# The conditioning nets' first layer moved up between x's first two weight blocks, with its tiles and the class table reordered on the load queue

## What is computed

```python
def _mlp_ln(s, W1, b1, W2, b2, g, b):
    h = jax.nn.silu(s @ W1 + b1) @ W2 + b2
    return _ln(h, g, b)

h = _ln(x, pw_g[pathway_ids], pw_b[pathway_ids])
h = _ln(h, cp_g[compartment_ids], cp_b[compartment_ids])
t = _ln(x, tm_g[time_steps], tm_b[time_steps])
m = x + _mlp_ln(memory_state, mem_W1, ...)[:, None, :]
n = x + _mlp_ln(noise_state, noi_W1, ...)[:, None, :]
r = x + _mlp_ln(resource_state, res_W1, ...)[:, None, :]
s = _ln(x, ms_g[scale_type], ms_b[scale_type])
w = softmax(aw)
cat = concatenate([w[0]*h, w[1]*t, w[2]*m, w[3]*n, w[4]*r, w[5]*s], axis=-1)
out = x + _mlp_ln(cat, int_W1, int_b1, int_W2, int_b2, int_g, int_be)
```

## Time and profile before

| | us |
|---|---|
| median of 3 runs | 929.16 |
| lowest and highest | 928.73, 929.22 |
| the profiled execution | 928.64 |
| its span in the trace | 926.9 |
| TensorE busy in the span | 919.0 |
| VectorE busy | 825.6 |
| ScalarE busy | 326.7 |
| GpSimd busy | 472.5 |

### The profile page before, as it was taken

One profiled execution on the slowest core, in us unless ns is written; L12 is line 12 of the kernel. 1 busy time (PEld: TensorE's weight loads), 2 busy tenths in 40 slices (PEclk: granted clock), 3 DMA queues, 4 the chain that ended last, 5 costly groups with the idle time before them and its releaser, 6 DMA issues.

```text
span 926.9 us, 13511 instructions
## 1 busy us (share of the span) xinstructions
PE 919.0 (99%) x4194; PEld 747.9 (81%) x4194; DVE 825.6 (89%) x1204; ACT 326.7 (35%) x415; POOL 472.5 (51%) x578
## 2 busy tenths in 40 slices
PE   9999999999999999999999999999999999999997
PEld 8777888888888888888888888888888888888885
DVE  7889999899898989989899898989989898998955
ACT  5835234252332514234242333424233251423412
POOL 5556473545545464563645546464563645446141
PEclk9999999999999999999999999999999999999999
DMA  9984757738566583856738465683856748475451
GB/s 333 358 307 148 227 163 244 196 89 279 154 206 179 164 267 102 254 142 234 197 112 281 139 214 161 197 244 91 268 139 239 182 137 276 120 241 145 126 114 45
DMA packets 99619, 178.75 MB, mean 193 GB/s; under 512 B 10129, under 2 KB 49041, under 8 KB 95633
## 3 DMA queue, kind: packets, MB, share of 16 engines
q1 hardware_dynamic: 44512, 95.88, 29.1%
q0 software_dynamic: 22976, 66.07, 27.9%
q10 hardware_dynamic: 32112, 16.58, 6.1%
HBM read 145.75 MB, written 32.75 MB: 193 GB/s over the span
## 4 chain that ended last, share of the span: by engine, by line
PE 97%; DVE 1%; DMA 1%; POOL 1%; ACT 0%; issue 0%; POOLq 0%; DVEq 0%; SPq 0%
PE hid_ps L1620 25%; PE hid_ps L1621 25%; PE hid_ps L1622 25%; PE o_ps L1707 3%; PE o_ps L1706 3%; PE made_ps L1707 3%; PE made_ps L1706 3%; PE o_ps L1708 3%; PE made_ps L1708 3%; PE made_ps L1563 1%; DMA keep<-int_W 1%; PE hid_ps L1627 0%; PE o_ps L1532 0%; PE o_ps L1520 0%; PE o_ps L1521 0%; PE o_ps L1548 0%
## 5 line engine op out<-in xcount | busy, mean ns | idle before, releaser
L1620 PE MATMUL hid_ps<-cat_hi,w_hi 128*128 128x512 f32 x1008 | 394.5, 391 | 0.0
L1622 PE MATMUL hid_ps<-cat_hi,w_lo 128*128 128x512 f32 x1008 | 392.3, 389 | 0.0
L1621 PE MATMUL hid_ps<-cat_lo,w_hi 128*128 128x512 f32 x1008 | 392.3, 389 | 0.0
L1620 PEld LDWEIGHTS hid_ps<-cat_hi,w_hi 128*128 128x128 f32 x1008 | 189.2, 188 | 46.2 <-issue 7.4
L1622 PEld LDWEIGHTS hid_ps<-cat_hi,w_lo 128*128 128x128 f32 x1008 | 189.2, 188 | 39.6
L1621 PEld LDWEIGHTS hid_ps<-cat_lo,w_hi 128*128 128x128 f32 x1008 | 189.3, 188 | 38.5
L617 POOL DMA_INDIRECT pw_rows<-pw,path_now x64 | 73.6, 1149 | 123.4 <-DVE y_sb L1147 106.6
L638 POOL DMA_DIRECT2D r_sb<-x x60 | 57.5, 958 | 108.2 <-DVE r_sb L1225 105.5
L853 ACT ACTIVATE cat_hi<-v_ring 128x1024 fp32r<-128x1024 f32 x30 | 31.9, 1062 | 201.2 <-DMA v_ring<-h_turned 201.2
L624 POOL DMA_INDIRECT pw_rows<-cp,class_now x64 | 84.1, 1313 | 32.7 <-issue 13.0
L845 ACT ACTIVATE cat_hi<-v_ring 128x1024 fp32r<-128x1024 f32 x64 | 66.4, 1059 | 84.1 <-DVE v_ring L1091 37.9
(11 more groups left out here) (199 smaller groups left out, 1385.4 us busy)
## 6 DMA issues: line engine op xcount, KB each, us to landing
x_sb<-xp SPq DMA_DIRECT2D x16, 1024.0 KB
out<-r_sb SPq DMA_DIRECT2D x63, 256.0 KB, 2.0
xc<-xT SPq DMA_DIRECT2D x15, 1024.0 KB, 9.3
h_turned<-y_sb ACTq DMA_DIRECT2D x60, 256.0 KB
r_sb<-x POOLq DMA_DIRECT2D x60, 256.0 KB, 4.2
v_ring<-h_turned SPq DMA_DIRECT2D x60, 256.0 KB
stats_bc<-token_stats SPq DMA_DIRECT2D x15, 512.0 KB
ids_sb<-ids SPq DMA_DIRECT2D x16, 256.0 KB
```

Source lines behind the costliest of these rows:

```text
L1620: pe.matmul(acc, w1_hi[:, k, cols], hi, start=start, stop=False)
L1621: pe.matmul(acc, w1_hi[:, k, cols], lo, start=False, stop=False)
L1622: return pe.matmul(acc, w1_lo[:, k, cols], hi, start=False, stop=stop)
```

## The change

- SyncE's list: the class table (`tabs`, 256 KB) now goes ahead of x^T's second half (512 KB), and the four NET tiles go straight behind it, so ahead of `keep_load(2)`, the ids, `keep_load(3)`, row_ids, blocks 4 and 5 and the kinds. Their wait for `stage_cleared` moves with them.
- TensorE: `nets_hidden` runs behind the second `warm` (13 instead of 15 matmuls) and ahead of `x_high_part(1)`; it writes `made_ps` instead of `o_ps` and doesn't wait for `xhat_copied` any more. `nets_hidden_turn`, which stays where it was, takes that wait. `first_fill(0)`, which writes `made_ps`, waits for `net_hid_rows`.
- ScalarE: the class table's two operations go ahead of `x_high(0, 1)`, and `nets_rows` from behind `w_high(5)` to between `sum_high(1)` and `sum_first(2)`.
- VectorE's new `x_moments`, behind `x_stats` of batch 0, makes variance plus EPS and minus the mean; GpSimd's part for batch 0 is left with two operations of four: the power, and the product with minus the mean.

```diff
-WARM = (30, 15)
+WARM = (30, 13)
...
             keep_load(1)
+            sp.dma_start(tab_raw, tabs).then_inc(table_in, 16)
             load_xT_half()
-            sp.dma_start(tab_raw, tabs).then_inc(table_in, 16)
+            for n in NET:
+                if tiles[n][1] < P:
+
+                    sp.wait_ge(stage_cleared, 1)
+                stage_load(n)
             keep_load(2)
...
-                nth = 1 if isinstance(b, int) and b == 0 else b + 2
-                rstd(xaggr, TT * (b + 1), xve, xve_done, xrs, xrs_done, xmv, slice(0, TT), nth)
                 if isinstance(b, int) and b == 0:
-
+                    pool.wait_ge(xve_done, 2)
+                    pool.tensor_tensor(xrs[:, :], xve[:, :], minus_half[:, :], ALU.pow).then_inc(xrs_done, 1)
                     pool.wait_ge(xrs_done, 1)
-                    pool.tensor_tensor(xmr[:, :], xmv[:, :, 0], xrs[:, :], ALU.mult).then_inc(xve_done, 1)
-                    pool.wait_ge(xve_done, 2)
-                    pool.tensor_tensor(xnmr[:, :], c_zero, xmr[:, :], ALU.subtract).then_inc(xrs_done, 1)
+                    pool.tensor_tensor(xnmr[:, :], xmr[:, :], xrs[:, :], ALU.mult).then_inc(xrs_done, 1)
                     return
...
+            def x_moments():
+                dve.wait_ge(xaggr, TT)
+                dve.wait_ge(half_ready, 6)
+                dve.tensor_tensor(xve[:, :], xmv[:, :, 1], eps_col[:, :], ALU.add).then_inc(xve_done, 1)
+                dve.tensor_scalar(xmr[:, :], xmv[:, :, 0], -1.0, None, ALU.mult).then_inc(xve_done, 1)
+
...
             def nets_hidden():
 
-                pe.wait_ge(xhat_copied, 2)
...
-                    pe.matmul(o_ps[at:at + 32, 0, :], sT[:, c, :], stage[NET[c] % STAGE], start=True, stop=True).then_inc(pe_used, 1)
+                    pe.matmul(made_ps[at:at + 32, 0, :], sT[:, c, :], stage[NET[c] % STAGE], start=True, stop=True).then_inc(pe_used, 1)
 
             def nets_hidden_turn():
-                pe.wait_ge(net_hid_rows, 1)
+                pe.wait_ge(xhat_copied, 2)
...
+                    pe.wait_ge(net_hid_rows, 1)
```

More of the change, by code:

```diff
@@ L467, in _ @@
             load_kinds(0)
[L468 to L472, removed]
             for i in range(FT + 2, FT + 6):
@@ L550, in x_rstd @@
                 wait(pool, pack_turned, b - 1)
-                nth = 1 if isinstance(b, int) and b == 0 else b + 2
-                rstd(xaggr, TT * (b + 1), xve, xve_done, xrs, xrs_done, xmv, slice(0, TT), nth)
                 if isinstance(b, int) and b == 0:
+                    pool.wait_ge(xve_done, 2)
+                    pool.tensor_tensor(xrs[:, :], xve[:, :], minus_half[:, :], ALU.pow).then_inc(xrs_done, 1)
                     pool.wait_ge(xrs_done, 1)
-                    pool.tensor_tensor(xmr[:, :], xmv[:, :, 0], xrs[:, :], ALU.mult).then_inc(xve_done, 1)
-                    pool.wait_ge(xve_done, 2)
-                    pool.tensor_tensor(xnmr[:, :], c_zero, xmr[:, :], ALU.subtract).then_inc(xrs_done, 1)
+                    pool.tensor_tensor(xnmr[:, :], xmr[:, :], xrs[:, :], ALU.mult).then_inc(xrs_done, 1)
                     return
+                rstd(xaggr, TT * (b + 1), xve, xve_done, xrs, xrs_done, xmv, slice(0, TT), b + 2)
                 pool.nop(nofuse=True)
@@ L777, in nets_rows @@
                 act.wait_ge(pe_used, count(PE_TILES, NET[-1]))
-                act.activation(net_h[:, :], o_ps[:, 0, :], ACT.Copy).then_inc(net_hid_rows, 1)
+                act.activation(net_h[:, :], made_ps[:, 0, :], ACT.Copy).then_inc(net_hid_rows, 1)
             def nets_silu():
@@ L886, in _ @@
             sum_first(1)
-            x_high(0, 1)
             act.wait_ge(table_in, 16)
@@ L891, in _ @@
             act.activation(class_tab[:, :], class_tab[:, :].bitcast(f32), ACT.Copy, scale=tab_sign).then_inc(tab_hi_done, 1)
+            x_high(0, 1)
             sum_high(1)
+            nets_rows()
             sum_first(2)
@@ L905, in first_chunk @@
                 w_high(5)
-                nets_rows()
                 w_high(6)
@@ L1328, in first_chunk @@
                     x_stats(0, t)
+                x_moments()
                 sum_blocks(1)
@@ L1735, in first_chunk @@
                 warm(WARM[1])
+                nets_hidden()
                 x_high_part(1)
```

1 line of the change is left out of this document (removed).

## The result

The changed kernel is slower by 1.2 us, a little over 0.1%: 929.98 us (median of 22 runs, 929.78 to 931.86) against 928.75 us for the kernel before (22 runs, 928.53 to 929.35), a ratio of 1.0013 with a 95% interval of 1.0007 to 1.0019. The profiled execution took 929.88 us, its span is 928.2 us against 926.9, at the same mean clock of 0.998.

What follows compares the result with a forecast made beforehand. TensorE, without waits from about 21 us, was taken to bound the kernel. Block 2 +1.34 us less the nets' 0.99 gave +0.35 on the 929.16 us median: 929.5 us, range 927.9 to 930.7.

Steps and rivals of the forecast that it cites:

- The wait that decides: ScalarE's `x_norm`, behind `sum_first(2)` and its load `keep_load(2)`, sets TensorE's block 2, which goes on 2.28 us behind x_norm's start.
- The landing of `keep_load(2)`: SyncE's queue: moved back by 704 KB of NET tiles, from 16.12 to 18.84 us, bounds 18.06 and 19.19.
- The nets' 0.99 us out of the gapless stretch: TensorE: the nets' four matmuls leave the part without waits, so `first_fill(1)` gains 0.99 us.
- The sum: Block 2's delay less the nets' gain on TensorE: +1.34 - 0.99 = +0.35 us.
- S: Start of `x_norm` on ScalarE, 18.15 before and forecast 19.49; TensorE's block 2 moves by S - 18.15.
- The nets' new place: TensorE behind 13 warms: nets from about 15.9 to 17.1, nearly free, in place of two warms and a wait.
- ScalarE's list: ScalarE with `nets_rows` ahead of `sum_first(2)`: by this list alone x_norm starts at 18.20, and the sum is -0.94 us.
- GpSimd's gain: GpSimd's `xnmr` done at 17.2, some 0.9 us earlier, with at most 0.52 us for the product.
- The load keeps its pace: Rival: `keep_load(2)` lands at 18.06 or better, giving -0.43 us, down to -0.94; chance 0.33.
- TensorE slows down: Rival: a TensorE wait longer than 0.59 us brings back the slow pace, costing another 1.9 us, +2.25 in all; chance 0.06.
- The NET tiles late: Rival: NET tiles landing beyond 17.2 cost a us each us; with others later still, +0.8 to +1.8, chance 0.08.
- The covers: Other moved loads, row_ids' gathers and waits cost nothing: `keep_load(3)` just in time at 22.02, third gather at 35.7.

## Why the prediction was right in its outcome and short in its size

It gave 929.5 us, +0.35 against the kernel before, and most of the chance to no change beyond 0.2%. The kernel is slower by 0.13%, so within that bound, but by 1.2 us and not by 0.35. The mechanism was the one named; one term was mis-sized. Part of the closeness of 929.5 to the 929.98 measured is luck: the median of three runs from which it starts, 929.16, lies 0.4 us above the 928.75 of 22 runs, and so hides nearly half of the 0.9 us by which the effect was too small. And +1.2 us lies in the band from +0.8 to +1.8, which had a chance of 0.08, not in the one to which 0.5 was given.

- **The wait that decides** (right): x_norm waits for `sum_first(2)` and that for `keep_load(2)`, and the last six transposes follow x_norm by 2.26 us (20.48 to 22.74), forecast 2.28.
- **The landing of `keep_load(2)`** (the step that failed): forecast 18.84, with 19.19 as the upper bound; it was 19.78. So the landing and x_norm's start (20.48, not 19.5) lie outside the signs written down for a right forecast, and TensorE's last wait, until 22.74, is one behind 22 us, which stood among the signs of a wrong one; it is the forecast wait for x_norm, only later. Of the 0.94 us between, 0.35 are the packet, of which I took 0.78 of 1.13 us by reading linearly between two landings. The loads are in flight when it comes, and they pay it whole; the runs without it showed 1.04 and 1.20 us. The other 0.6 us were in no bound: I priced all 704 KB at the pace of tiles that fill 128 partitions, and two of the four don't. The run with the same bytes on 128 partitions showed 0.6, and its landing, 19.19, is the forecast's upper bound. The trace of the kernel before had held this already: from 22.0 to 23.5 us, where by the bytes that the queue had moved these two tiles were due, it moved 0.10, 0.10 and 0.15 MB per half microsecond.
- **The nets' 0.99 us out of the gapless stretch** (right): 2.31 - 1.29 = 1.02. It is the only thing that the change gains.
- **The sum.** With the landing as it was, the prediction's own working gives S = 19.81 + 0.71 - 0.09 = 20.43, +2.28 - 0.99 = +1.29 us, which is what the span grew by (+1.3).
- **The nets' new place** (right): they ran from 16.47 to 17.9, and the forecast was 15.85 to 17.1. The first warm took 9.76 us instead of 8.96 (written the same way, it took from 8.34 to 9.76 us in the profiles of this case), and the last tile landed at 16.8, 0.8 later than reckoned, for the same two small tiles. Block 1 started at 17.80 instead of 17.2, which cost nothing, since behind it stood a wait anyway.
- **ScalarE's list** (right): `sum_high(1)` from 16.48 to 17.11, forecast 16.53 to 17.16. By this list alone S would have been near the 18.20 reckoned.
- **GpSimd's gain** (too large, without effect): the product took 1.14 us, so xnmr was ready at 17.75 and not at 17.2.
- **The load keeps its pace** (chance 0.33): fell. The chance was too high for a rival against which two rows of the trace spoke.
- **TensorE slows down** (0.06): TensorE waited 1.3 us, in pieces of 0.51, 0.38 and 0.38 with one or two transposes between, and the matmuls behind them kept their duration (1.17 and 1.07 us for four). Waits of this kind did no harm; a single wait as long as their sum didn't occur here. In the run with the loads' order alone the first piece was 1.21 us, and the matmuls behind it took 1.17 and 1.08 us as well.
- **The NET tiles late** (part of 0.08): the last landed at 16.8, under the 17.2 from which it would cost.
- **The covers**: all held. `sum_first(3)` ran from 23.11, right behind `sum_high(2)`. The third gather was issued at 28.1 and landed at 37.3, later than the 35.7 forecast, and its reader started at about 39.1, since VectorE was later too. TensorE doesn't wait behind the last six transposes.

The Trainium skill ("Runtime: NRT & Kernel Launch", Instruction fetch mechanics) calls the cost of crossing an instruction block "mostly hidden". For TensorE itself the two traces agree: behind its first instruction, all the waits listed for it are for ScalarE, in both kernels. But the loads in flight paid 1.04 to 1.20 us, and in the changed kernel TensorE waited, by way of ScalarE, for one of them.

## What to carry to other kernels

Price a load in a busy queue by the queue's pace and by its shape: the tiles on 64 and 32 partitions took about as long as a full one of twice their bytes, for everything queued behind them, so stack small weight tiles over all partitions. When work is moved into an idle spot, ask first what its loads push back: here they pushed back the one load with a waiting reader by 3.7 us, to gain 1.0 us of TensorE. A jump between two landings that holds an instruction packet was to be taken whole here, and a few wide filler instructions in place of many narrow ones moved that packet to where no load was awaited.

## What the runs showed of the hardware that I had not expected

- Loads onto part of the partitions are slow with the engines shown as busy: about 0.10 to 0.11 MB per half microsecond for tiles on 64 and 32 partitions against 0.19 for 128, and 235 GB/s over the stretch from 15.0 to 16.5 us against 386 to 407 in the runs without such tiles; with one tile of 96 partitions it was 318. The Trainium skill ("SBUF — State Buffer", Door 1: The DMA port swizzle) says that the bandwidth depends on how many of 16 ports the partitions reach, and that partitions 0 to 31 and 32 to 63 lie on the same half of them. This case's rows agree with the half.
- One instruction packet of 0.02 MB made the next loads of the queue land about 1.1 us later (1.04, 1.13 and 1.20), as much as its own time of 1.13 us, while the bytes moved per half microsecond fell by 0.01 MB or not at all. It came between 15.5 and 18.0 us in the eight kernels with the narrow first warm, and between 25.0 and 26.5 in the four where that warm had 88 records of matmuls and weight loads fewer. Further down the queue of the kernel before the difference grew: the kinds landed at 22.78 us with the packet and at 21.10 without it. Why it grew wasn't tried.
- GpSimd's product of 128x4 values took 1.14 us where a subtraction of the same size took 0.52 and another product 0.36. What the difference comes from wasn't tried.
